# A decoder layer on one core: the order of side jobs, vector steps and SP's DMAs changed within a batch

## What is computed

```
x  = layernorm(x + self_attention(x))
x1 = x                                     # 16 heads of 16
q, k, v = x1 @ Wq.T, ctx @ Wk.T, ctx @ Wv.T
out = softmax(where(mask, q k.T / 4, -inf)) v
x2 = layernorm(x1 + out @ Wo.T)
base = x2 @ W_base + b_base
recon_n = relu(x2 @ W_enc[n] + b_enc[n]) @ W_dec[n] + b_dec[n]      # 8 experts
n = argmin over experts of mean((recon_n - x2)^2), one for each batch
y = base + relu(x2 @ W_down[n] + b_down[n]) @ W_up[n] + b_up[n]
return layernorm(x2 + y)
```

## Time and profile before

| what | us |
|---|---|
| median of 3 runs | 1651.06 (1650.19 to 1655.74) |
| profiled execution, its own time | 1650.58 |
| its span, first to last instruction | 1648.8 |
| PE busy | 1586.7 (96%) |
| DVE busy | 1238.2 (75%) |
| ACT busy | 1053.2 (64%) |
| GpSimd (POOL) busy | 161.2 (10%) |

### The profile page before, as it was taken

One profiled execution on the slowest core, in us unless ns is written; L12 is line 12 of the kernel. 1 busy time (PEld: TensorE's weight loads), 2 busy tenths in 40 slices (PEclk: granted clock), 3 DMA queues, 4 the chain that ended last, 5 costly groups with the idle time before them and its releaser, 6 DMA issues.

```text
span 1648.8 us, 25559 instructions
## 1 busy us (share of the span) xinstructions
PE 1586.7 (96%) x9632; PEld 588.7 (36%) x9632; DVE 1238.2 (75%) x1790; ACT 1053.2 (64%) x1998; POOL 161.2 (10%) x151
## 2 busy tenths in 40 slices
PE   6779999999999999999999999999999999999997
PEld 5442323332333333332333323433333323332233
DVE  5788777877788777887888777887778777887522
ACT  2227776676666666676666766676666776666661
POOL 7311000100011000100001000110001000000000
PEclk8899999999999999999999999999999999999999
DMA  5655071623517071442707163361707234150010
GB/s 156 116 143 101 25 138 41 101 69 86 96 40 127 28 131 40 90 93 62 116 22 134 32 113 69 69 112 52 121 12 122 61 52 77 50 78 5 11 33 16
DMA packets 118663, 125.22 MB, mean 76 GB/s; under 512 B 35186, under 2 KB 100339, under 8 KB 118540
## 3 DMA queue, kind: packets, MB, share of 16 engines
q1 hardware_dynamic: 117724, 123.06, 38.3%
q10 hardware_dynamic: 816, 0.53, 0.1%
HBM read 84.18 MB, written 35.03 MB: 72 GB/s over the span
## 4 chain that ended last, share of the span: by engine, by line
PE 85%; DVE 7%; ACT 3%; issue 3%; DMA 1%; SPq 0%; POOL 0%; POOLq 0%; DVEq 0%; ACTq 0%
PE banks L1122 23%; PE values L1141 23%; PE banks L1082 12%; PE work L1012 5%; PE work L998 5%; PE work L957 4%; DVE xneg_max_pieces L1439 4%; PE work L1019 3%; PE work L1025 3%; ACT xprobs L1260 3%; PE work L1004 2%; PE work L1028 1%; PE work L942 1%; PE work L1037 1%; DMA max_dram<-xneg_max_rows 1%
## 5 line engine op out<-in xcount | busy, mean ns | idle before, releaser
L1260 ACT ACTIVATE xprobs<-banks 128x512 f32<-128x512 f32 x1664 | 900.5, 595 | 408.3 <-PE banks L1122 405.0
L1439 DVE TENSOR_REDUCE xneg_max_pieces<-banks 128x2 f32<-128x1024 f32 x768 | 909.0, 1219 | 258.4 <-PE banks L1082 257.2
L1122 PE MATMUL banks<-xq_stacks,xk_stacks 99*128 99x512 bf16 (+1 forms) x1664 | 517.7, 385 | 9.9 <-ACT xprobs L1260 3.0
L1141 PE MATMUL values<-xprobs,xv_rows 128*17 128x512 f32 x3328 | 437.9, 598 | 1.3 <-ACT xprobs L1260 1.3
L1122 PEld LDWEIGHTS banks<-xq_stacks,xk_stacks 99*128 99x128 bf16 (+1 forms) x1664 | 127.4, 97 | 398.8 <-ACT xprobs L1260 273.2
L1082 PE MATMUL banks<-xk_stacks,xq_stacks 49*128 49x512 bf16 (+1 forms) x2048 | 250.3, 335 | 14.2 <-DVE xneg_max_pieces L1439 12.3
L1082 PEld LDWEIGHTS banks<-xk_stacks,xq_stacks 49*128 49x128 bf16 x2048 | 57.2, 94 | 327.6 <-DVE xneg_max_pieces L1439 212.9
L1510 POOL TENSOR_TENSOR xk_parts<-xk_rest,xk_parts 128x401 bf16<-128x401 f32 (+1 forms) x64 | 59.0, 923 | 660.5 <-ACT xk_parts L1239 660.5
L1141 PEld LDWEIGHTS values<-xprobs,xv_rows 128*17 128x17 f32 x3328 | 55.1, 95 | 122.9 <-issue 117.6
L1505 POOL TENSOR_TENSOR xrstd<-xrstd,mhalf 128x4 f32<-128x4 f32 x23 | 23.2, 1011 | 652.4 <-DVE xrstd L1314 652.4
L1012 PEld LDWEIGHTS work<-xvT,ctxT_a 128*128 128x128 f32 (+1 forms) x416 | 54.3, 192 | 13.6 <-issue 3.9
(11 more groups left out here) (295 smaller groups left out, 1007.3 us busy)
## 6 DMA issues: line engine op xcount, KB each, us to landing
xk_stacks<-key_parts_dram SPq DMA_DIRECT2D x186, 200.1 KB, 13.0
key_parts_dram<-xk_parts SPq DMA_DIRECT2D x144, 100.0 KB, 2.2
xq_stacks<-parts_dram SPq DMA_DIRECT2D x186, 64.0 KB, 8.8
ctxT_a<-in_ctxT SPq DMA_DIRECT2D x4, 1601.0 KB, 7.5
ctxT_b<-in_ctxT SPq DMA_DIRECT2D x4, 1601.0 KB, 7.5
parts_dram<-xq_parts SPq DMA_DIRECT2D x45, 128.0 KB, 2.0
key_parts_dram<-xk_parts SPq DMA_DIRECT2D x48, 100.2 KB, 5.2
xa<-in_x SPq DMA_DIRECT2D x8, 512.0 KB, 16.3
```

Source lines behind the costliest of these rows:

```text
L1122: pe.matmul(at, kst[0:ROWS[par], k, h2, par, t * P:(t + 1) * P], qst[0:ROWS[par], k, h2, par, :], start=True, stop=True).then_inc(made, 1)
L1141: last = pe.matmul(av[32 * j:32 * j + HD + 1, :], vals[:, k, t, gr * GH + j, :], probs[:, sl % 2, j, :], start=t == 0, stop=t == XKT - 1)
L1260: nc.scalar.activation(probs[:, sl % 2, j, :], score_bank(n)[0], ACT.Exp).then_inc(exped, 1)
L1439: nc.vector.tensor_reduce(nmp[:, of % 2, :, j2, q, piece], pairs[n % MRING][:, :, :], AX.X, ALU.max, negate=True).then_inc(on["mxr"], 1)
```

## The change

The tables `IN_BETWEEN`, `SLOT_END` and `VECTOR_WORK` and the order of SP's and GpSimd's programs are edited; no matmul, vector operation or DMA is added or dropped.

- In between: x1T 1 goes from slot 11 to 12, x2T 1 from 16 to 15, the loss from 35 to 34. v 3 is no longer in between (slot 18) but the end job of slot 14, in one part.
- End jobs: v 2 goes from slots 14 and 15 to 10 and 11; enc 0 from 16 and 17 to 15 and 16; kproj 2 and 3 from 10 and 11 to 17 and 20; enc 1 from 20 and 21 to 21 and 22; kproj 4 from 22 to 25; enc 2 from 25 and 26 to 26 and 27; gram 2 from three parts in 27 to 29 to two in 28 and 29. The others stay in their slots.
- Vector steps: in slot 5 the scaling of group 3 of the batch before comes ahead of the norm's two steps; the choose steps go from slots 35 to 37 to slots 34 to 36.
- SP stores the parts of qproj 0 ahead of move_outputs(m) and spread_inverses(m), and those of kproj 2 and 3 behind these. GpSimd makes qproj 0's low part ahead of those of kproj 2 and 3.

```diff
--- before.py
+++ after.py
@@ -830,17 +830,16 @@
 
         NOW, NEXT, PREV = 0, 1, -1
         IN_BETWEEN = {
-            8: ("x1T", 0, NEXT), 11: ("x1T", 1, NEXT), 14: ("x2T", 0, PREV), 16: ("x2T", 1, PREV), 18: ("v", 3, NOW),
-            35: ("loss", 0, PREV),
+            8: ("x1T", 0, NEXT), 12: ("x1T", 1, NEXT), 14: ("x2T", 0, PREV), 15: ("x2T", 1, PREV), 34: ("loss", 0, PREV),
         }
         SLOT_END = [
             (("kproj", 0, NEXT), 1), (("kproj", 1, NEXT), 1), (("v", 0, NOW), 2), (("v", 1, NOW), 2),
-            (("xo", 0, PREV), 2), (("xo", 1, PREV), 2), (("kproj", 2, NEXT), 1), (("kproj", 3, NEXT), 1),
-            (("qproj", 0, NEXT), 2), (("v", 2, NOW), 2), (("enc", 0, PREV), 2), (("gram", 0, PREV), 2),
-            (("enc", 1, PREV), 2), (("kproj", 4, NEXT), 1), (("gram", 1, PREV), 2), (("enc", 2, PREV), 2),
-            (("gram", 2, PREV), 3), (("enc", 3, PREV), 2), (("gram", 3, PREV), 2), (("kproj", 5, NEXT), 1),
-            (("kproj", 6, NEXT), 1), (("kproj", 7, NEXT), 1), (("v", 4, NEXT), 2), (("v", 5, NEXT), 2),
-            (("mid", 0, PREV), 2), (("y", 0, PREV), 2), (("y", 1, PREV), 2), (("v", 6, NEXT), 2),
+            (("xo", 0, PREV), 2), (("xo", 1, PREV), 2), (("v", 2, NOW), 2), (("qproj", 0, NEXT), 2),
+            (("v", 3, NOW), 1), (("enc", 0, PREV), 2), (("kproj", 2, NEXT), 1), (("gram", 0, PREV), 2),
+            (("kproj", 3, NEXT), 1), (("enc", 1, PREV), 2), (("gram", 1, PREV), 2), (("kproj", 4, NEXT), 1),
+            (("enc", 2, PREV), 2), (("gram", 2, PREV), 2), (("enc", 3, PREV), 2), (("gram", 3, PREV), 2),
+            (("kproj", 5, NEXT), 1), (("kproj", 6, NEXT), 1), (("kproj", 7, NEXT), 1), (("v", 4, NEXT), 2),
+            (("v", 5, NEXT), 2), (("mid", 0, PREV), 2), (("y", 0, PREV), 2), (("y", 1, PREV), 2), (("v", 6, NEXT), 2),
             (("qproj", 1, NEXT), 2), (("v", 7, NEXT), 1),
         ]
         AT_END = [(job, part, parts) for job, parts in SLOT_END for part in range(parts)]
@@ -862,11 +861,11 @@
             27: [("invert", "o", 1, NOW)], 32: [("scale", "o", 1, NOW)],
             40: [("invert", "o", 2, NOW)], 44: [("scale", "o", 2, NOW)],
             2: norm_steps("stats", "x1", 0, 2, NEXT), 3: norm_steps("stats", "x1", 2, 4, NEXT),
-            5: [*norm_steps("apply", "x1", 0, 2, NEXT), ("scale", "o", 3, PREV)],
+            5: [("scale", "o", 3, PREV), *norm_steps("apply", "x1", 0, 2, NEXT)],
             6: norm_steps("apply", "x1", 2, 4, NEXT), 8: norm_steps("stats", "x2", 0, 2, PREV),
             9: norm_steps("stats", "x2", 2, 4, PREV), 10: [("aggr", "x2", 0, PREV)],
             11: norm_steps("apply", "x2", 0, 2, PREV), 12: norm_steps("apply", "x2", 2, 4, PREV),
-            35: choose_steps(0, 4), 36: choose_steps(4, 8), 37: choose_steps(8, CHOOSE_STEPS),
+            34: choose_steps(0, 4), 35: choose_steps(4, 8), 36: choose_steps(8, CHOOSE_STEPS),
             45: norm_steps("stats", "y", 0, 2, PREV), 47: norm_steps("stats", "y", 2, 4, PREV),
             48: [("aggr", "y", 0, PREV)], 49: norm_steps("apply", "y", 0, 2, PREV),
             50: norm_steps("apply", "y", 2, 4, PREV),
@@ -1529,9 +1528,9 @@
             if prev:
                 pool_rstd("x2", b - 1)
             if nxt:
+                pool_qlow(0, b + 1)
                 pool_klow(2, b + 1)
                 pool_klow(3, b + 1)
-                pool_qlow(0, b + 1)
                 for i in range(4, 8):
                     pool_klow(i, b + 1)
             if prev:
@@ -1706,12 +1705,12 @@
                 sp_store_x1(nxt)
             sp_max_rows(m + 1)
             if nxt < B:
+                sp_query_parts(0, uses_before(0, nxt))
+            sp_move_outputs(m)
+            sp_spread_inverses(m)
+            if nxt < B:
                 sp_key_parts(2, use + 2)
                 sp_key_parts(3, use + 3)
-            sp_move_outputs(m)
-            if nxt < B:
-                sp_query_parts(0, uses_before(0, nxt))
-            sp_spread_inverses(m)
             sp_max_rows(m + 2)
             if nxt < B:
                 sp_free_key_dram(nxt, 1)
```

## The result

The changed kernel takes 1695.62 us (median of 4 runs, 1693.84 to 1696.13), the kernel before 1650.67 (1650.19 to 1655.74): a ratio of 1.0263, with a 95% interval of 1.0242 to 1.0285. It is slower, as forecast, but by 45 us where I had said 23. The profiled execution took 1695.57, its span is 1693.8.

What follows compares the result with a forecast made beforehand. The prediction took PE as the bound, with at most 0.71 us a batch to win by better order. Its terms, together 23.4 us on top of 1650.6, gave 1674 us, with a range from 1655 to 1687.

Steps and rivals of the forecast that it cites:

- What bounds the kernel: Middle batches: PE is busy 188.31 of 189.02 us, so better order wins at most 0.71 us a batch.
- Matmul work: Slots 10 to 35: v3 gets its own slot, gram 2 shrinks to two slots; +0.22 us a batch.
- Scale before apply: Slot 5: PE gets 0.5 us in slot 6 and gives it back by slot 8; 0.
- Transposes in slot 12: Slot 11's 0.23 wait goes, slot 12 waits 0.43, qrest in slot 13 is 0.1 late; +0.3 us.
- Query parts ahead of the moves: DVE's invert in slot 14 waits for later output moves, delaying PE in slot 16; +0.9 us a batch, 2.3 in batch 0.
- kproj 4 in slot 25: Context ahead of the moves delays DVE in slot 27, PE in slot 29; +1.9 us in batches 1 to 5, 2.7 in batch 0.
- upper bound from the attention rows: Slot 29: moves land 2 us behind the context, as a small load did behind a large one; 3.3 us a batch.
- The stacks 2.4 us later: Key stacks start some 2.4 us later but are wanted only in slot 35, where PE is later too; 0.
- (a): Rival: the context doesn't hold the moves, only slot 14's wait is left; 1662 us, chance 0.16.
- (b): Rival: neither DVE wait, slot 14's or slot 27's, reaches PE; 1652 to 1655 us, no difference, chance 0.14.
- (c): Rival: faster, slot 6's 0.5 us is kept in 6 batches and no new wait comes; 1645.6 us, chance 0.07.
- (d): Rival: moves land at V26 (slot 26's start) + 13 or later, 1686 us, or slot 35 misses stacks, over 1690; chance 0.13.

Runs made afterwards that it cites:

- both behind: Changed kernel with the query parts put back behind move_outputs(m) and the context load behind move_outputs(m+1), job tables as changed: 1675.7 us, ratio 1.0139.
- context behind the moves: Changed kernel with the load of the context issued behind move_outputs(m+1) instead of ahead of it: 1685.2 us, ratio 1.0199.
- before, context held: Kernel before, with SP waiting for slot 26's evacuation before it issues the context, ahead of move_outputs(m+1): 1662.6 us, ratio 1.0061.
- four extra matmuls: Changed kernel with four matmuls of unused result added ahead of slot 29's max pairs in batches 0 to 5: 1684.5 us, ratio 1.0194.

## Why the prediction was right in sign and short in size

- **What bounds the kernel**: right. PE's waits decide; the middle slots' content costs the same wherever it stands.
- **Matmul work, +0.22 a batch**: right. Slot 14 (v3 alone with transposes) has 4.08, slot 29 without its wait 4.22, the loss costs nearly the same in its new slot. With the SP orders put back the batches have +0.2 (batch 6 of "both behind": +0.21). That is +0.23 for v3 and gram 2, less 0.1 for each of the next two points, and +0.2 of small things that the sum had at nothing: 0.08 in slot 26 behind kproj 4, 0.07 for x2T 1 in its new slot, 0.05 for the loss.
- **Scale before apply, 0**: right within 0.1, by the trace and by the run of that part alone. The 0.5 of slot 6 is given back in slots 7 and 8.
- **Transposes in slot 12, +0.3**: too high. Slots 11 and 12 have 3.44 and 4.14, so the new wait is 0.1 and not 0.5, and the net is -0.1. Batch 1's slot 12 has 0.7 more in this trace, a wait for late max rows.
- **Query parts ahead of the moves, +0.9 and 2.3 in batch 0**: right in kind. Measured 0.66 to 0.68 in batches 3 to 6, 1.6 and 1.2 in batches 1 and 2, 3.5 in batch 0: together 8.9, where the sum had 7.7. In batches 3 to 6 DVE goes at V14 + 7.9 as worked out, and PE first has to wait for it 0.2 later than the sum had; in batches 1 and 2 DVE goes at 8.8 and 8.5. Of batch 0's 3.5, 1.3 stand in slot 17, at the lower clock. Undoing it alone gave 7.7 us.
- **kproj 4 in slot 25, +1.9 and 2.7 in batch 0**: this is the step that failed. The mechanism is right, the size is not, and this term is more than the whole error (24.8 us, where the forecast was 21.6 short). Slots 29 and 30 of batches 0 to 5 have 37.0 us over the matmul content, the sum had 12.2. Three things make the difference. (1) DVE goes at V26 + 13.3 on average, not 11.0, which is worth 13.9 us in six batches. Of these 2.3, 0.55 is ACT's evacuation, which stands ahead of kproj 4's middle part in slot 26 and only there; my time for the low part was from slot 22, where no evacuation is. The rest is the landing of the moves behind the context, 9.2 to 10.9 from its issue instead of 8.05. That is 2 us beyond "the context without its last latency", as my own upper bound from the attention rows had it. (2) With the wait so long PE's granted clock fell to 0.7 to 0.8 over slot 29. I had no term for that; by the relation above it costs 13.4 us, 2.2 a batch. (3) The other way, PE first has to wait when DVE goes at V26 + 9.4 and not at 9.05 (in batch 0 at 9.3 and not at 8.3), so the term was 2.6 too high for its own 11.0. 12.2 + 13.9 + 13.4 - 2.6 = 36.9.
- **The stacks 2.4 us later, 0**: right for the changed kernel, since PE is later too. But the slack is small: in batch 3 of "both behind" slot 38 is 2.2 longer with SP going on at V38 + 2.5, so it can come as late as V38 + 0.3; in the kernel before it comes at V38 - 3.8. That is about 4 us of slack in a middle batch; in batch 0 slot 38 waits already in the kernel before (4.45). As soon as slot 29's wait is taken away, slot 38's comes (runs "context behind the moves" and "both behind"). The prediction treated the hold as a matter of order in the queue. The context's 1.6 MB, moved from a stretch in which the DMA engines had little else to do (in the changed kernel, which loads no context there, their share is 0.02 in slots 23 and 24 and 0.09 in 25 and 26) into the stretch ahead of the stacks, is the cost, and it comes out at one place or the other.
- **Rivals**: (a), the context doesn't hold the moves, is refuted by "before, context held": DVE goes 3 to 4 us later by the context's place alone. (b) and (c) fell. (d) had the size (moves at V26 + 13 or later), though not the clock: its 1686 is still 10 short. That the direction came out right is no luck, as slot 16's excess and slot 29's stand where they were forecast.

The sum of the known parts: 37.0 (slots 29, 30) + 8.9 (query parts) + 0.7 (slot 12 of batch 1) + 1.8 (all else in the loop) = 48.4, less 3.35 in the front of this execution. Why the front was shorter isn't settled; it is untouched code, and the loop begins anywhere from 122.0 to 129.9 us in the traces of all the runs.

No version beat the kernel before. Its PE stands idle 0.71 us a period, and the parts of the change that win anything (slot 11's wait, slot 6's) win 0.2 a batch together.

## What to carry to other kernels

A large load has a place in time, not only in a queue's order. Here one that was made to wait for an earlier instruction of its queue came to lie in front of small, urgent DMAs, and held them, by some 3 us even from another queue. For each wait that a reordering delays, list what is queued or under way behind it, with its bytes. And price a wait of the bound engine above its length: waits of 2.0 to 4.0 us cost another 1.6 to 3.0 us each here, because the matmuls behind them ran at a lower clock.

## What was unexpected in the hardware

- In the changed kernel and its repetition PE waits 2.0 to 4.0 us for DVE within slot 29 of batches 1 to 5 and 0.5 to 0.7 once more. The granted clock was 0.69 to 0.82 over the slot, and pairs of records of the float32 products behind the waits took 1.35 to 1.91 us instead of 1.02 (full speed is 2.4 GHz, the lower level 1.2). Where slot 29 was 5.6 to 6.3 long, in the run with the context on ACT's queue, its waits were 0.4 to 1.1 and 0.7, and the clock stayed at 1.00. The view of stretches of the changed kernel, slot 29 of batches 1, 4 and 6:

```profile
411.58:422.74 11.16, 6.66 (x21) 0.69 0.60 92
...
1000.60:1011.80 11.20, 7.22 (x22) 0.72 0.61 105
...
1392.52:1396.74 4.22, 4.22 (x21) 1.00 0.18 44
```

- A second queue helped hardly at all: with the context on ACT's queue and the moves on SP's, DVE was released 8.6 to 9.3 us after the context's issue, with both on SP's queue 8.3 to 9.5 ("before, context held") or 9.2 to 10.9 (changed kernel). Without a context the moves landed 1.4 us after their last issue.
- One float32 matmul of 128x512 shows as two records of 0.59 us each that overlap, and takes 0.86 us of PE (the four extra matmuls of slot 29 are eight records, one every 0.43 us).
